# Cross-attention: V's parts in one stationary operand, four context products a step

## The chip, the cores and the metric

One core of a Trainium2 chip runs the whole kernel as one program. The time is the device time of one execution in microseconds (us), as the median of several. Of the engines, PE is TensorE (matrix products; PEld is its loading of the stationary operand), DVE is VectorE, ACT is ScalarE, POOL is GpSimd, and SP issues most of the DMAs.

## The reference

A decoder block on x of 32 sequences x 256 tokens x 256 columns: self-attention, cross-attention to a context of 120 tokens, and a mixture of 16 experts, each followed by a residual sum and a layer norm. The change touches cross-attention alone:

```
q = einsum('bsd,dhk->bshk', x, Wq);  k, v = the same of ctx with Wk, Wv      # 16 heads of 64
logits  = einsum('bthk,bfhk->bhft', k, q * 64**-0.5)
weights = softmax(logits, axis=-1)
ctx     = einsum('bhft,bthk->bfhk', weights, v)
out     = einsum('bfhk,hkd->bfd', ctx, Wo)
```

## The kernel before

Every fp32 product is computed from rounded parts. A value is split into a high part (its copy in the format that PE reads, made by ACT) and a low part (the value minus the high part, made by DVE), and `three` (L127 to L131) replaces one product by three: high by high, low by high and high by low. In the trace these are lines L129, L130 and L131.

**Stages.** Self-attention comes first, cross-attention second, the experts last. Cross-attention works in steps: a step g is one pair of heads of one sequence, so there are 8 steps (NP) a sequence and 256 in all. The step's work is software-pipelined over slots: in slot m each engine does, for several different steps, the part that is due there. The offsets are written out by hand (L872): queries and keys at m - 2 (QL), scores and exponentials at m - 4 (SL), reciprocal and normalisation at m - 5 (IL), transposes of the probabilities at m - 6 (TL), the context product at m - 8 (CL), the output product at m - 10 (OL). One slot a step, so the length of a slot is what 256 steps cost. The functions `tensor`, `scalar`, `vector`, `gpsimd` and `sync` inside `cross_attention` each hold a `slot(J, m)`: it issues that engine's instructions of slot m in this order, and an engine runs them in that order. A body has 32 slots (four sequences) and runs eight times. The first slots of the stage lie among the last ones of self-attention, and the last ones among the first work of the experts.

**What a slot holds beside the steps' own work.** Keys are computed for two sequences at once, so the key products (six), ACT's and DVE's two key passes each (on partitions 0 to 63 and 64 to 127) stand in eight slots of sixteen only. V is projected in slots 1 and 2 of each eight (six products of 512 columns each). The residual, the norm, the transposes of x and x2 and the gate have their places by m modulo 8, and each body has the choice of tokens (softmax over experts, four rounds of the eight largest).

**The context product before.** V lies in SBUF as `v_hi` and `v_lo` (L806), for each pair of heads 64 columns of head 0, 64 of zeros and 64 of head 1. A window of 128 columns holds head 0 and zeros, or zeros and head 1; with it as stationary operand and the transposed probabilities `pT_hi`, `pT_lo` (256 columns) as moving one, the two heads' three products each (six in all, L1079) add up in one region of the bank `CX`, `CX[:, 0:T]`, in which head 0 has partitions 0 to 63 and head 1 has 64 to 127. PE starts them when the low part of step g - 1 has been read from `CX` (`cxlo_done`, L1076). ACT copies `CX` to `c_hi` (L1180), DVE subtracts that from `CX` to make `c_lo` (L1286), both in slot g + 8, and PE's output product reads both in slot g + 10 (L1117).

**Order in a slot.** PE: V projection, scores, transposes of x, keys and queries, context product, transposes of the probabilities, x2 transposes, gate, output product. ACT: xT, `v_hi`, `q_hi`, `k_hi`, `c_hi`, `pT_hi`, x2T, gate, four exponentials with their sums (L1206). DVE: xT, `v_lo` (L1249), residual (L1256), maximum (`ca_shift`, L1262), reciprocal (`ca_inverse`, L1268), `q_lo` (L1275), `k_lo` (L1279), `c_lo`, `pT_lo` (L1291), x2, statistics, the choice of tokens. The bank of queries and keys is single: PE's next queries wait for `q_lo` and `k_lo` of the step before.

## Time and profile before

| | us |
|---|---|
| median of three runs | 3175.88 (3175.04 to 3178.29) |
| profiled execution: its span, first to last instruction | 3171.4 |
| PE busy | 3088.7 (97%) |
| DVE busy | 2256.1 (71%) |
| ACT busy | 2142.4 (68%) |
| POOL busy | 1581.9 (50%) |

The page gives the profiled execution by its span; what lies around the span isn't in it (the median of the runs is 4.5 us above it). Busy time is the union of an engine's instructions. On DVE and ACT an instruction's recorded time includes a tail in which the next one already runs, so what an instruction costs in a row of them is the distance from its start to the next one's start, which is shorter than its own time. On PE likewise: products overlap in the records, and the distance of their starts is their cost.

### The profile page before, as it was taken

How to read it: one execution, taken by the hardware profiler on the slowest of the kernel's cores; microseconds unless marked ns; L12 is line 12 of the kernel's file. 1: busy time of each engine (PE TensorE's matmuls, PEld its weight loads, DVE VectorE, ACT ScalarE, POOL GpSimd, SP SyncE). 2: the span in 40 equal slices, each digit the busy share in tenths (PEclk: the TensorE clock that was granted, in tenths of full speed). 3: DMA queues.
4: the chain of work that ended last, by engine and by line, in shares of the span. 5: the costliest groups of instructions: out<-in, count | busy, mean ns of one | idle time of the engine just before them, and what ended most of it. 6: DMA issues, size and time to landing. Idle time of an engine off the chain costs nothing. (4 is left out here: it accounts for less than half of the span.)

```text
span 3171.4 us, 78666 instructions
## 1 busy us (share of the span) xinstructions
PE 3088.7 (97%) x22624; PEld 2900.2 (91%) x22624; DVE 2256.1 (71%) x6566; ACT 2142.4 (68%) x6930; POOL 1581.9 (50%) x2904
## 2 busy tenths in 40 slices
PE   6999999999999998999999999999989999999998
PEld 5999999999999987999999999999868888889998
DVE  6777777777877877778877778787745455544665
ACT  6888888888887877787877877777734444442222
POOL 3666766766676765333333333333446666653000
PEclk8999999999999999999999999999989999999999
DMA  6444444444444440121111111111245444533333
GB/s 181 117 120 125 127 125 121 121 120 122 127 111 111 125 143 24 48 64 45 54 55 45 57 55 44 64 45 48 94 118 119 100 98 101 128 56 85 120 124 106
DMA packets 193684, 300.70 MB, mean 95 GB/s; under 512 B 33856, under 2 KB 134080, under 8 KB 192704
## 3 DMA queue, kind: packets, MB, share of 16 engines
q1 hardware_dynamic: 168768, 262.91, 27.8%
q0 software_dynamic: 24576, 33.57, 6.2%
q8 instruction: 176, 2.88, 0.4%
q14 instruction: 164, 1.34, 0.1%
HBM read 116.02 MB, written 67.11 MB: 58 GB/s over the span
## 5 line engine op out<-in xcount | busy, mean ns | idle before, releaser
L964 POOL TENSOR_SCALAR ca_prob<-ca_prob,ca_inverse 128x120 f32<-128x120 f32 x1024 | 354.6, 365 | 632.5 <-DVE ca_inverse L1268 630.5
L665 ACT ACTIVATE sa_prob<-sa_prob,sa_shift 128x128 f32<-128x128 f32 (+1 forms) x1024 | 453.6, 461 | 2.6 <-DVE sa_shift L718 2.6
L1206 ACT ACTIVATE ca_prob<-bank,ca_shift 128x120 f32<-128x120 f32 x1024 | 353.7, 366 | 6.0 <-DVE ca_shift L1262 3.5
L460 POOL TENSOR_SCALAR sa_prob<-sa_prob,sa_inverse 128x128 f32<-128x128 f32 x512 | 198.5, 388 | 234.5 <-DVE sa_inverse L726 220.4
L718 DVE CUSTOM_DVE_ANT_0 sa_prob<-bank,sa_mask 128x128 f32<-128x128 f32 (+1 forms) x1024 | 304.7, 352 | 6.9 <-PE bank L138 2.7
L136 PE MATMUL bank<-sa_ow,sa_y_hi 128*128 128x256 f32 x1024 | 279.6, 304 | 0.0
L136 PE MATMUL bank<-sa_kvT_a,sa_q 128*128 128x128 f32 (+1 forms) x1024 | 251.7, 281 | 17.7 <-DMA sa_q<-sa_q_tile 17.4
L138 PE MATMUL bank<-sa_kvT_b,sa_q 112*128 112x128 f32 (+1 forms) x1024 | 261.6, 281 | 0.0
L749 DVE TENSOR_TENSOR sa_pT_lo<-bank,sa_pT_hi 128x384 fp32r<-128x384 f32 x512 | 258.3, 544 | 1.8 <-ACT sa_pT_hi L650 1.8
L138 PE MATMUL bank<-sa_ow,sa_y_lo 112*128 112x256 f32 x1024 | 258.8, 283 | 0.0
L462 POOL TENSOR_SCALAR sa_prob<-sa_prob,sa_inverse 128x256 f32<-128x256 f32 x512 | 244.9, 478 | 0.0
L1824 ACT ACTIVATE ex_act_g<-bank 128x512 f32<-128x512 f32 x128 | 76.5, 598 | 239.5 <-PE bank L131 226.0
L1677 POOL DMA_INDIRECT mid_acc<-ex_out,ex_to_tokens x112 | 191.1, 1706 | 88.1 <-DVE ex_out L1939 56.3
L742 DVE TENSOR_TENSOR sa_y_lo<-bank,sa_y_hi 96x512 fp32r<-96x512 f32 x256 | 175.1, 684 | 71.8 <-ACT sa_y_hi L642 61.6
L650 ACT ACTIVATE sa_pT_hi<-bank 128x384 fp32r<-128x384 f32 x512 | 223.2, 494 | 3.1 <-PE bank L565 2.9
L642 ACT ACTIVATE sa_y_hi<-bank 128x512 fp32r<-128x512 f32 x256 | 153.0, 598 | 99.0 <-PE bank L131 99.0
L1206 ACT ACTIVATION_READ_ACCUMULATOR ca_prob<-bank,ca_shift 128x1 f32 x1024 | 219.4, 214 | 0.0
L136 PEld LDWEIGHTS bank<-sa_kvT_a,sa_q 128*128 128x128 f32 x1024 | 197.5, 193 | 19.1 <-issue 18.1
L565 PE MATMUL bank<-all_ident,sa_prob 128*128 128x128 f32 x1536 | 211.4, 274 | 3.0 <-POOL sa_prob L462 2.9
L1906 DVE TENSOR_TENSOR ex_hid<-ex_act_g,bank 128x512 f32<-128x512 f32 x128 | 87.8, 686 | 175.0 <-PE bank L131 165.3
L665 ACT ACTIVATION_READ_ACCUMULATOR sa_prob<-sa_prob,sa_shift 128x1 f32 x1024 | 210.7, 206 | 0.0
L731 DVE SCALAR_TENSOR_TENSOR sa_q_tile<-bank,sa_qbias,sa_q_tile 128x512 fp32r<-128x512 f32 x144 | 107.7, 748 | 142.4 <-ACT sa_q_tile L633 142.3
(259 smaller groups left out, 12014.1 us busy)
## 6 DMA issues: line engine op xcount, KB each, us to landing
sa_q<-sa_q_tile SPq DMA_DIRECT2D x128, 288.0 KB
sa_q<-sa_q_tile SPq DMA_DIRECT2D x160, 112.0 KB
mid_x2T<-ca_x2T SPq DMA_DIRECT2D x32, 512.0 KB, 3.0
ex_sx<-mid_x2T SPq DMA_DIRECT2D x32, 512.0 KB, 3.3
sa_q<-sa_q_tile SPq DMA_DIRECT2D x304, 32.0 KB, 3.0
sa_xT_raw<-in_xT SPq DMA_DIRECT2D x32, 256.0 KB, 2.8
sa_q<-sa_q_tile SPq DMA_DIRECT2D x32, 256.0 KB
sa_x_res<-in_x SPq DMA_DIRECT2D x32, 256.0 KB, 2.8
```

What stands on the lines that cost most here:

```text
L136: pe.matmul(out, stat_hi, mov_hi, start=start, stop=False, skip_group_check=True)
L138: return pe.matmul(out, stat_lo[rows], mov_lo[rows], start=False, stop=stop, skip_group_check=True)
L460: pool.tensor_scalar(prob[:, r, hh, 0:P], prob[:, r, hh, 0:P], inverse[:, r, 2 * hh:2 * hh + 1], 1.0, ALU.mult, ALU.mult)
L462: pool.tensor_scalar(prob[:, r, hh, P:3 * P], prob[:, r, hh, P:3 * P], inverse[:, r, 2 * hh + 1:2 * hh + 2], 1.0, ALU.mult, ALU.mult).then ...
L565: mm = pe.transpose(TR[hh][:, n * P:n * P + P], prob[:, r, hh, n * P:n * P + P], ident[:])
L650: act.activation(pT_hi[:, r, hh], TR[hh][:, 0:3 * P], ACT.Copy).then_inc(pThi_done, 1)
L665: act.activation(prob[:, r, hh, cols], prob[:, r, hh, cols], ACT.Exp, bias=shift[:, r, n:n + 1], scale=-1.0, accum_out=total[:, r, n:n + 1 ...
L718: dve.tensor_tensor_reduce(out=prob[:, r, hh, cols], in0=SC[hh][:, t * T:t * T + (t + 1) * P], in1=mask[:].rearrange("p a s -> p (a s)")[: ...
L749: dve.tensor_tensor(pT_lo[:, r, hh], TR[hh][:, 0:3 * P], f32(pT_hi[:, r, hh]), ALU.subtract).then_inc(pTlo_done, 1)
L964: ins = pool.tensor_scalar(prob[:, r, t, hh], prob[:, r, t, hh], inverse[:, r, n:n + 1], 1.0, ALU.mult, ALU.mult)
L1206: act.activation(prob[:, r, t, hh], SC[g % 2][:, n * S:n * S + S], ACT.Exp, bias=shift[:, r, n:n + 1], accum_out=total[:, r, n:n + 1]).the ...
L1677: pool.indirect_dma_start(d["acc"].rearrange("b t c -> (b t) c"), bass.IndirectOffsetOnAxis(ap=of[:, j:j + 1], axis=0), out[:, i, t], None ...
```

## The change

V's four parts of a pair of heads lie in one tensor `v`, side by side: high part of head 0, low of head 0, low of head 1, high of head 1, 64 columns each, without zeros. One stationary operand of 128 columns holds high and low part of one head; it is multiplied with `pT_hi` and with `pT_lo`. So there are two products a head, four a step. The two halves of the result lie on different partitions, head 0 in columns 0 to 255 of `CX` and head 1 in columns 256 to 511. ACT copies the whole of `CX` (512 columns) to a new tensor `cx`. DVE then makes two sums on 64 partitions each, of one half from `CX` and the other half from `cx`, into a new tensor `c`. At the head of the next slot ACT rounds `c` to `c_hi` and DVE subtracts, `c_lo = c - c_hi`, now with both inputs in SBUF. PE's next context product waits for the sums (`csum_done`), its output product for `c_lo` (`chalf_lo`). ACT makes `v`'s high parts in one pass of 512 columns and DVE its low parts in one, where there were two of 256 columns. GpSimd no longer writes the zeros of V.

```diff
@@ -56,6 +56,7 @@
 MASKED = -3e38
 SELF_SCALE = float(C // H) ** -0.5
 CROSS_SCALE = float(DH) ** -0.5
+PAST_LOW = 576
 
 
 Later = namedtuple("Later", "own base")
@@ -803,7 +804,10 @@
     xT_hi, xT_lo = al.split("xT", [P, 2, KC, T])
     q_hi, q_lo = al.split("q", [P, RING, T])
 
-    v_hi, v_lo = al.split("v", [S, 2, NP, 3 * DH])
+    al.sb("v_before", [P, PAST_LOW])
+    cx = al.sb("cx", [P, 2, 2 * T])
+    al.sb("v_between", [P, 4 * T - PAST_LOW])
+    v = al.sb("v", [S, 2, NP, 4, DH], F32R)
     k_hi, k_lo = al.split("k", [P, 2, NP, 2 * S])
     prob = al.sb("prob", [P, RING, TT, 2, S])
     shift = al.sb("shift", [P, RING, TT * 2])
@@ -829,6 +833,7 @@
     var_eps, rstd = al.sb("var_eps", [P, TT]), al.sb("rstd", [P, TT])
 ...
+    c = al.sb("c", [P, 2, T])
 
     XT, M, QK, SC, TR, CX, O = *bank[0:3], bank[3:5], *bank[5:8]
 
@@ -858,7 +863,8 @@
     s_mm, max_done, exp_done = al.sem("s_mm"), al.sem("max_done"), al.sem("exp_done")
     inv_done, p_done = al.sem("inv_done"), al.sem("p_done")
     p_tr, pThi_done, pTlo_done = al.sem("p_tr"), al.sem("pThi_done"), al.sem("pTlo_done")
-    cx_mm, cxhi_done, cxlo_done = al.sem("cx_mm"), al.sem("cxhi_done"), al.sem("cxlo_done")
+    cx_mm, cxcopy_done, csum_done = al.sem("cx_mm"), al.sem("cxcopy_done"), al.sem("csum_done")
+    chalf_hi, chalf_lo = al.sem("chalf_hi"), al.sem("chalf_lo")
 ...
@@ -936,12 +942,11 @@
             pool.wait_ge(cross.o_mm, B * NP)
             pool.wait_ge(cross.w_lo, KC * (len(CROSS) - 1))
             pool.memset(half[:], -0.5).then_inc(const, 1)
-            zeros = [k_hi[0:DH, :, :, S:2 * S], k_lo[0:DH, :, :, S:2 * S], k_hi[DH:P, :, :, 0:S], k_lo[DH:P, :, :, 0:S],
-                     v_hi[:, :, :, DH:2 * DH], v_lo[:, :, :, DH:2 * DH]]
+            zeros = [k_hi[0:DH, :, :, S:2 * S], k_lo[0:DH, :, :, S:2 * S], k_hi[DH:P, :, :, 0:S], k_lo[DH:P, :, :, 0:S]]
             for n, t in enumerate(zeros):
                 pool.wait_ge(const, n + 1)
                 pool.memset(f32(t), 0.0).then_inc(const, 1)
-            pool.wait_ge(const, 7)
+            pool.wait_ge(const, 5)
 ...
@@ -987,7 +992,7 @@
 
     def tensor(pe):
 
-        first_use = {1: (cross.w_lo, KC), QL: (cross.w_lo, KC * (len(CROSS) - 1)), SL: (const, 5), QL + 1: (cross.o_read, B), CL: (const, 7),
+        first_use = {1: (cross.w_lo, KC), QL: (cross.w_lo, KC * (len(CROSS) - 1)), SL: (const, 5), QL + 1: (cross.o_read, B),
                      OL: (cross.w_lo, KC * (len(CROSS) - 1) + 1), GATE: (gate_done, 1)}
 
         def slot(J, m):
@@ -1073,11 +1078,12 @@
                 if p == 0:
                     need(pe, vlo_done, upto_seq(J, g // NP, 2))
                 need(pe, pTlo_done, upto(J, g))
-                need(pe, cxlo_done, upto(J, g - 1))
+                need(pe, csum_done, upto(J, g - 1, 2))
                 for hh in range(2):
-                    win = slice(hh * DH, hh * DH + 2 * DH)
-                    mm = three(pe, CX[:, 0:T], v_hi[:, b, p, win], v_lo[:, b, p, win], pT_hi[:, r, hh], pT_lo[:, r, hh],
-                               hh == 0, hh == 1)
+                    both = v[:, b, p, 2 * hh:2 * hh + 2].rearrange("s a k -> s (a k)")
+                    out = CX[:, hh * T:(hh + 1) * T]
+                    pe.matmul(out, both, pT_hi[:, r, hh], start=True, stop=False, skip_group_check=True)
+                    mm = pe.matmul(out, both, pT_lo[:, r, hh], start=False, stop=True, skip_group_check=True)
                 mm.then_inc(cx_mm, 1)
             g = m - TL
             if step_exists(J, g):
@@ -1114,7 +1120,7 @@
             g = m - OL
             if step_exists(J, g):
                 r, p = g % RING, g % NP
-                need(pe, cxlo_done, upto(J, g))
+                need(pe, chalf_lo, upto(J, g))
                 if p == 0:
                     need(pe, o_read, upto_seq(J, g // NP - 1))
                 for t in range(TT):
@@ -1128,6 +1134,11 @@
 
     def scalar(act):
         def slot(J, m):
+            g = m - CL - 1
+            if step_exists(J, g):
+                need(act, csum_done, upto(J, g, 2))
+                need(act, o_mm, upto(J, g - RING))
+                act.activation(c_hi[:, g % RING], c[:, g % 2], ACT.Copy).then_inc(chalf_hi, 1)
             if m % (2 * NP) == 0 and seq_exists(J, m // NP):
                 pr = m // (2 * NP)
                 need(act, c_in, upto_pair(J, pr, 32))
@@ -1154,10 +1165,8 @@
                 need(act, v_mm, upto_seq(J, b, 2, n - 1))
                 if n == 0:
                     need(act, cx_mm, upto(J, (b - 1) * NP - 1))
-                for hh in range(2):
-                    ins = act.activation(v_hi[:, b % 2, n * NP // 2:(n + 1) * NP // 2, hh * 2 * DH:hh * 2 * DH + DH],
-                                         v_bank(J, b, n)[0:S, :].rearrange("s (p h k) -> s p h k", h=2, k=DH)[:, :, hh], ACT.Copy)
-                ins.then_inc(vhi_done, 1)
+                act.activation(v[:, b % 2, n * NP // 2:(n + 1) * NP // 2, 0:4:3],
+                               v_bank(J, b, n)[0:S, :].rearrange("s (p h k) -> s p h k", h=2, k=DH), ACT.Copy).then_inc(vhi_done, 1)
             g = m - QL
             if step_exists(J, g):
                 r, b, p = g % RING, (g // NP) % 2, g % NP
@@ -1174,10 +1183,9 @@
                     ins.then_inc(khi_done, 1)
             g = m - CL
             if step_exists(J, g):
-                r = g % RING
                 need(act, cx_mm, upto(J, g))
-                need(act, o_mm, upto(J, g - RING))
-                act.activation(c_hi[:, r], CX[:, 0:T], ACT.Copy).then_inc(cxhi_done, 1)
+                need(act, csum_done, upto(J, g - 2, 2))
+                act.activation(cx[:, g % 2], CX[:], ACT.Copy).then_inc(cxcopy_done, 1)
             g = m - TL
             if step_exists(J, g):
                 r = g % RING
@@ -1226,6 +1234,10 @@
 
     def vector(dve):
         def slot(J, m):
+            g = m - CL - 1
+            if step_exists(J, g):
+                need(dve, chalf_hi, upto(J, g))
+                dve.tensor_tensor(c_lo[:, g % RING], c[:, g % 2], f32(c_hi[:, g % RING]), ALU.subtract).then_inc(chalf_lo, 1)
             if m % (2 * NP) == 0 and seq_exists(J, m // NP):
                 need(dve, chi_done, upto_pair(J, m // (2 * NP)))
                 dve.tensor_tensor(cT_lo[:], cT_raw[:], f32(cT_hi[:]), ALU.subtract).then_inc(clo_done, 1)
@@ -1244,11 +1256,9 @@
                 if isinstance(J, int) and J == 0 and m == 1:
                     dve.wait_ge(cross.o_mm, B * NP)
                 need(dve, vhi_done, upto_seq(J, b, 2, n - 1))
-                for hh in range(2):
-                    at = (slice(None), b % 2, slice(n * NP // 2, (n + 1) * NP // 2), slice(hh * 2 * DH, hh * 2 * DH + DH))
-                    ins = dve.tensor_tensor(v_lo[at], v_bank(J, b, n)[0:S, :].rearrange("s (p h k) -> s p h k", h=2, k=DH)[:, :, hh],
-                                            f32(v_hi[at]), ALU.subtract)
-                ins.then_inc(vlo_done, 1)
+                of = v[:, b % 2, n * NP // 2:(n + 1) * NP // 2]
+                dve.tensor_tensor(of[:, :, 1:3], v_bank(J, b, n)[0:S, :].rearrange("s (p h k) -> s p h k", h=2, k=DH),
+                                  f32(of[:, :, 0:4:3]), ALU.subtract).then_inc(vlo_done, 1)
             if m % NP == NORM % NP and seq_exists(J, (m - NORM) // NP):
                 b = (m - NORM) // NP
                 need(dve, o_mm, upto(J, (b + 1) * NP - 1))
@@ -1281,9 +1291,12 @@
                     ins.then_inc(klo_done, 1)
             g = m - CL
             if step_exists(J, g):
-                r = g % RING
-                need(dve, cxhi_done, upto(J, g))
-                dve.tensor_tensor(c_lo[:, r], CX[:, 0:T], f32(c_hi[:, r]), ALU.subtract).then_inc(cxlo_done, 1)
+                need(dve, cxcopy_done, upto(J, g))
+                need(dve, chalf_lo, upto(J, g - 2))
+                for hh in range(2):
+                    own, other = slice(hh * DH, (hh + 1) * DH), slice((1 - hh) * DH, (2 - hh) * DH)
+                    dve.tensor_tensor(c[own, g % 2], CX[other, hh * T:(hh + 1) * T], cx[own, g % 2, hh * T:(hh + 1) * T],
+                                      ALU.add).then_inc(csum_done, 1)
             g = m - TL
             if step_exists(J, g):
                 r = g % RING
```

## Rows read from the trace of the kernel before

**Rows 1.** The page: busy time of the engines; the granted clock in 40 slices.

```profile
PE 3088.7 (97%) x22624; PEld 2900.2 (91%) x22624; DVE 2256.1 (71%) x6566; ACT 2142.4 (68%) x6930; POOL 1581.9 (50%) x2904
...
PEclk8999999999999999999999999999989999999999
```

**Rows 2.** Windows of the stage (stretch, length, busy of engines, clock, DMA share, GB/s).

```profile
1350.00:2154.00 804.00, 798.91 (x6574) 776.35 (x6573) 639.59 (x1715) 638.83 (x2483) 281.49 (x790) 1.00 0.16 52
1240.00:2290.00 1050.00, 1042.53 (x8576) 1012.63 (x8574) 833.13 (x2213) 836.14 (x3243) 377.62 (x1046) 1.00 0.17 55
```

**Rows 3.** Waits, 1350 to 2154 us (who waited for whom: total, times, longest).

```profile
ACT ca_q_hi L1166 <- PE bank L131: 115.3, 136, 1.4
DVE ca_q_lo L1275 <- ACT ca_k_hi L1172: 69.2, 78, 1.7
DVE ca_v_lo L1249 <- ACT ca_v_hi L1158: 41.8, 42, 1.5
...
PE bank L129 <- ACT ca_prob L1206: 5.1, 5, 1.3
```

**Rows 4.** Groups of DVE and ACT, 1350 to 2154 us (count, busy, mean ns, idle before).

```profile
L1286 DVE TENSOR_TENSOR ca_c_lo<-bank,ca_c_hi 128x256 fp32r<-128x256 f32 x192 | 80.8, 421 | 11.8 <-ACT ca_c_hi L1180 7.3
...
L1180 ACT ACTIVATE ca_c_hi<-bank 128x256 fp32r<-128x256 f32 x191 | 73.3, 384 | 30.9 <-PE bank L131 28.4
```

**Rows 5.** Timeline of PE (start, us): first of six context products, then transposes.

```profile
1629.63 0.29 PE L129 MATMUL bank<-ca_pT_hi,ca_v_hi 120*128 120x256 f32 x1
...
1630.34 0.60 PE L1089 MATMUL bank<-all_ident,ca_prob 128*120 128x128 f32 x4
```

**Rows 6.** Timeline of DVE in a slot with keys.

```profile
1617.81 0.42 DVE L1275 TENSOR_TENSOR ca_q_lo<-bank,ca_q_hi 128x256 fp32r<-128x256 f32 x1 [0.44 <-ACT ca_k_hi L1172]
1618.15 0.81 DVE L1279 TENSOR_TENSOR ca_k_lo<-bank,ca_k_hi 64x240 fp32r<-64x240 f32 x2
1618.99 0.42 DVE L1286 TENSOR_TENSOR ca_c_lo<-bank,ca_c_hi 128x256 fp32r<-128x256 f32 x1
1619.34 0.68 DVE L1291 TENSOR_TENSOR ca_pT_lo<-bank,ca_pT_hi 120x512 fp32r<-120x512 f32 x1
1619.93 0.68 DVE L1314 TENSOR_TENSOR ca_x2T<-bank,ca_x2T 128x512 fp32r<-128x512 f32 x1
```

**Rows 7.** Timeline of DVE: V's two low parts; the chosen tokens' columns, by partitions.

```profile
1607.45 0.76 DVE L1249 TENSOR_TENSOR ca_v_lo<-bank,ca_v_hi 120x256 fp32r<-120x256 f32 x2 [1.48 <-ACT ca_v_hi L1158]
1608.12 0.68 DVE L1256 TENSOR_TENSOR ca_res<-bank,ca_x_res 128x512 f32<-128x512 f32 x1
...
1661.89 0.18 DVE L1370 COPY all_weight_of<-bank 32x16 f32 x1
1661.98 0.23 DVE L1372 TENSOR_SCALAR all_token_of<-bank,ca_first_token 32x16 f32 x1
1662.22 0.18 DVE L1370 COPY all_weight_of<-bank 32x16 f32 x1
```

**Rows 8.** Timeline of ACT: from the context's copy to the exponentials' end.

```profile
1630.87 0.39 ACT L1180 ACTIVATE ca_c_hi<-bank 128x256 fp32r<-128x256 f32 x1
1631.15 0.59 ACT L1186 ACTIVATE ca_pT_hi<-bank 120x512 fp32r<-120x512 f32 x1
1631.63 0.36 ACT L1206 ACTIVATE ca_prob<-bank,ca_shift 128x120 f32<-128x120 f32 x1
...
1632.97 0.63 ACT L1143 ACTIVATE ca_xT_hi<-bank 128x512 fp32r<-128x512 f32 x1
```

**Rows 9.** Timeline of DVE in a slot without keys.

```profile
1655.35 0.42 DVE L1286 TENSOR_TENSOR ca_c_lo<-bank,ca_c_hi 128x256 fp32r<-128x256 f32 x1 [0.27 <-ACT ca_c_hi L1180]
...
1657.63 0.66 DVE L1262 TENSOR_REDUCE ca_shift<-bank 128x4 f32<-128x480 f32 x1 [0.94 <-PE bank L131]
```

**Rows 10.** Windows at the end of self-attention, in which the clock fell.

```profile
1162.00:1165.50 3.50, 0.85 (x5) 0.41 (x4) 1.77 (x11) 0.96 (x6) 3.19 (x8) 1.00 0.89 264
1165.50:1172.30 6.80, 5.70 (x25) 5.61 (x26) 1.96 (x6) 3.33 (x11) 1.25 (x3) 0.50 1.03 399
```

## The prediction, made before the changed kernel was timed

> **What bounds the kernel now.** I read the busy line and the clock first: PE is busy 97% of the span, at full clock but for a few slices [rows 1]. The change lies in one stage, so I then cut out that stage. From 1240 to 2290 us PE is busy 1042.5 of 1050 us at a clock of 1.00 [rows 2], and the longest sum of PE's own waits is 5.1 us in 804 [rows 3]. PE sets the pace. But the other two aren't far: in 804 us that hold 192 steps [rows 2, 4], a step takes 4.19 us, of which PE is busy 4.16, DVE 3.33 and ACT 3.33. So DVE and ACT have 0.86 us of room a step each, and this is the number that decides. The waits say what kind of idle time that room is: DVE waits 69 us for `k_hi` and 42 us for `v_hi`, and ACT waits 115 us for the query products [rows 3]. That is waiting for input from PE, in the slots in which PE has extra products. It isn't room that DVE can use whenever it likes.
>
> **PE: two products of six go.** The six start at 1629.63 and the transposes behind them at 1630.34: 0.71 us, 0.118 each [rows 5]. The four that stay have the same shape (120 rows of 128, 256 columns moving), so a step loses 0.24 us and PE needs 4.19 - 0.24 = 3.95. If nothing else moved, 256 steps would give 61 us.
>
> **DVE: one pass becomes three.**
> - The old `c_lo` goes, 1618.99 to 1619.34, 0.35 us [rows 6].
> - The new `c_lo` is as wide but reads two SBUF tensors. Its price in SBUF isn't in these rows; passes from the bank of the same width cost 0.34 and 0.35 [rows 6]. I take the same, between 0.30 and 0.42 (its whole recorded time, nothing overlapped). So the two cancel.
> - Two sums of 64 partitions by 256 columns come. The nearest row is the pair of `k_lo`, also 64 partitions each, also first 0 to 63 and then 64 to 127: from 1618.15 to the next start at 1618.99, 0.84 us for 2 x 240 columns [rows 6]. Two passes on 120 partitions that don't change partitions take less, 0.67 for 2 x 256 (`v_lo`, 1607.45 to 1608.12) [rows 7]. So the price of such a pair hangs not on the elements but on the step from one set of partitions to another. The small writes of the chosen tokens say the same: on one set of 32 partitions the next instruction starts 0.09 us behind, and where the set changes 0.24 us behind, when the one before has ended [rows 7]. The sums change partitions twice in a slot, like `k_lo`, so I take 0.84 plus 16 columns each at (0.68 - 0.42)/256, about 1 ns a column: 0.87 us. Bounds: 0.67 (as `v_lo`) and 0.95 (each its full time and a little more, since input and output of one instruction start at different partitions, which no row shows).
> - V's low parts in one pass of 512 columns cost as `pT_lo`, 0.59 [rows 6], for 0.67 [rows 7]: 0.08 less, twice in eight steps, 0.02 a step.
>
> Sum: 3.33 - 0.35 + 0.35 + 0.87 - 0.02 = 4.18 us of busy DVE a step, and 3.98 to 4.33 between the bounds. In steps without keys the same change of partitions newly falls behind `q_lo`. The Trainium skill ("VectorE: DVE Perf Modes", "Two Vector instructions with no wait between them") says that a Vector instruction starts only when all earlier ones have finished if its output, or its first input from SBUF or PSUM, starts in another group of 32 partitions than the last one did. The pairs in [rows 7] agree (0.09 and 0.24). It speaks against this change: it makes all passes around the sums dear, and by it `q_lo` too would be held in half of the steps, 0.08 more there, so that the sum would be 4.22 instead of 4.18.
>
> **ACT.** The copy grows from 256 to 512 columns: from 0.28 (1630.87 to 1631.15) to 0.48 (as `pT_hi`, 1631.15 to 1631.63) [rows 8]. The rounding of `c` is a pass more, 0.28. V's high parts in one pass save 0.02. Sum: 3.33 + 0.20 + 0.28 - 0.02 = 3.79; bounds 3.70 to 3.90 (recorded times instead of distances). ACT stays below PE's 3.95.
>
> **GpSimd** writes no zeros for V, once, before the first context product. Nobody is late for it: cost nothing on either side. SBUF and DMAs keep their order; SP's queue isn't touched.
>
> **The sum.** PE 3.95, DVE 4.18, ACT 3.79, against a step of 4.19. PE's saving is real and DVE takes its place as the bound, at a work that is nearly the length of the old step. A busy DVE isn't a DVE without idle time, and here is where I choose. Recorded tails make the 4.18 a little too large (ahead of each idle gap stands the tail of the last pass, 0.07 us for `c_lo`, 0.42 recorded against 0.35 to the next start [rows 6]; with one such gap a step, 4.11 is the hard floor, and I take 4.15). Against this stands idle time that can't be filled. In slots with the V projection PE has six products of 512 columns more, and DVE waits for `v_hi`, up to 1.5 us, 1.0 us in the mean of 42 waits [rows 3]. DVE can come late from the slot before and so use part of that: how late is set by the single banks. PE's next queries need `k_lo` at once, its next context product needs the sums, its next transposes need `pT_lo`; I take half a microsecond in slots without keys (there DVE waits 0.94 us before the maximum today [rows 9], less the longer copy) and a quarter or less in those with. So of the 1.0 us about half stays idle, in a quarter of the slots: 0.12 a step. The long slots of DVE (statistics, and the choice of tokens, of which the columns alone take four times the 0.33 us from 1661.89 to 1662.22 [rows 7]) exceed PE's and delay PE directly. The work's 4.15 plus 0.12 gives 4.27 a step.
>
> What is queued behind the new waits: at the head of a slot DVE now waits for ACT's `c_hi`, which ACT issues only behind its four exponentials (1.34 us, 1631.63 to 1632.97 [rows 8]) and only when DVE's sums are done. Behind that wait on DVE stand `v_lo`, the residual and the maximum, and the next exponentials wait for the maximum. The loop is `c_hi` 0.39, `c_lo` 0.42, maximum 0.66, exponentials 1.34: 2.8 us with the recorded times [rows 4, 6, 8, 9], shorter than any step, so it costs nothing in plain slots.
>
> 4.27 - 4.19 = 0.08 us a step. Of 256 steps I count 250 (the first and last ones lie among other work). 0.08 x 250 = 20 us. The profiled execution's span of 3171.4 would become 3191; the median of the runs is 4.5 above that span: 3195 to 3196, I say 3195.
>
> **The rivals.**
> - PE stays the bound. If the sums cost 0.67 or less and overlap as `v_lo`, DVE needs 3.98, beside PE's 3.95; with the V slots' idle time filled this is a step of 4.05 to 4.13: 15 to 35 us faster, 3141 to 3161. For it: PE has all its work ready, and 0.24 us is 6% of a step. Against it: `k_lo`. Chance 0.22, with all cases down to 3170.
> - It evens out. DVE at 4.18 to 4.20 with next to no idle time: 3170 to 3182. Chance 0.18. That is also what would be seen if the two products were saved and all of it lost to a full DVE.
> - My forecast, DVE is the bound with some idle time: 4.22 to 4.40 a step, 3182 to 3228, likeliest 3195. Chance 0.48.
> - The wait at the head of the slot makes ACT and DVE take turns. It decides once ACT's exponentials end later than DVE's `pT_lo` and extras: in slots with a fifth ACT pass (x2T, gate, xT) and keys. Each such slot then loses up to `c_hi`'s 0.39; in half of the slots that is 0.2 a step on top of my 4.27: 3195 + 50 = 3245. Chance 0.08.
> - The clock. It fell to 0.50 after 3.5 us in which PE was busy for 0.85 us, and stayed there for 6.8 us, with 5.7 busy [rows 10]. In the stage PE has no such gap today. The choice of tokens adds 1.3 us or more to DVE (four times 0.33 [rows 7]) in a slot in which PE could be short of work. One fall a body, 3.4 us at half speed, is 14 to 27 us more: 3209 to 3222. Chance 0.04.
>
> The Trainium skill ("SBUF — State Buffer", "SBUF: two separate sides") has another rule against the change: a VectorE instruction with two SBUF inputs and a GpSimd one that reads SBUF exclude each other. The new `c_lo` is of that kind. In numbers of this case: POOL is busy 281.5 of 804 us in 790 instructions [rows 2], 35% of the time and 0.36 us each. If they met by chance, 0.35 x 0.36/2 = 0.06 us a step, 16 us more, or some 3211, within the forecast's range; but `c_lo` comes after `pT_lo`, when the multiplies behind the reciprocal should be over. No row of the stage shows it; I give it 0.03 as the case by itself that moves the time up, out of the forecast's share.
>
> **How the numbers follow.** Chances: faster by over 0.2% (6.4 us, about what can be told from no change here) 0.22; within it 0.18; slower 0.48 + 0.08 + 0.04 = 0.60. The range leaves out about 0.1 on each side: from 3150 (a step of 4.09, just under DVE's floor) to 3236 (a step of 4.43, the upper bound of DVE's work and 0.1 of idle time). The likeliest case's own range is 3182 to 3228.
>
> **What would show it.** In the profile after, in the same stage: PE busy no longer 99% but 92 to 96%, with waits for the sums, `k_lo` or `pT_lo`; DVE busy 96% or more of the step and 4.1 to 4.2 us of it; ACT 3.8 us. The pair of sums, with the next start behind it, 0.84 to 0.90 us. PE's four products 0.47. DVE waits at `c_lo` for ACT's `c_hi` would be the turn-taking rival. I am wrong on the side of faster if the sums overlap (0.67) or DVE can run later behind PE than half a microsecond, and the step is then nearer to PE's 3.95.

## The result, and the profile after

The changed kernel takes 3211.85 us in the median (3210.27 to 3213.2), the kernel before 3176.52 beside it: a ratio of 1.0111 (95% interval 1.0097 to 1.0126), 35.3 us slower. The forecast was slower, 3195, so the sign and the range hold and the size is about half of what came. A second comparison on another chip gave 1.0123 (1.0107 to 1.014), 38.6 us; the experiments below are set against that one.

The page after, with the two lines that answer to [rows 1]:

```profile
span 3208.9 us, 78973 instructions
...
PE 3079.1 (96%) x22112; PEld 2854.2 (89%) x22112; DVE 2453.9 (76%) x7014; ACT 2256.4 (70%) x7122; POOL 1585.8 (49%) x2902
...
DVE  6787777777787778999999999999955555554565
...
PEclk8999999999999999999999999999989999999999
```

PE has 512 products fewer and only 9.6 us less busy time; DVE has 198 us more and now shows 9 tenths through nearly the whole stage, as PE did before. The stage's windows and groups, as in [rows 2, 4]:

```profile
1240.00:2330.00 1090.00, 1033.20 (x8082) 966.46 (x8082) 1030.00 (x2658) 951.68 (x3439) 381.81 (x1046) 1.00 0.17 54
1350.00:2154.00 804.00, 764.50 (x6000) 715.20 (x6000) 761.17 (x1978) 701.72 (x2548) 274.70 (x764) 1.00 0.16 51
...
L1298 DVE TENSOR_TENSOR ca_c<-bank,ca_cx 64x256 f32<-64x256 f32 x372 | 157.1, 422 | 11.8
L1304 DVE TENSOR_TENSOR ca_pT_lo<-bank,ca_pT_hi 120x512 fp32r<-120x512 f32 x186 | 128.7, 692 | 5.7
L1240 DVE TENSOR_TENSOR ca_c_lo<-ca_c,ca_c_hi 128x256 fp32r<-128x256 f32 x185 | 77.2, 417 | 3.6 <-ACT ca_c_hi L1141 3.2
```

The 372 sums are 186 steps, against 192 in the same 804 us before: a step takes 804/186 = 4.32 us, not 4.19. DVE is busy 761.17/186 = 4.09 of it, ACT 3.77, PE 4.11. PE's 4.11 isn't its work: 764.50 us for 6000 products are 0.127 us each, against 0.122 before (798.91 for 6574). I take the difference for pauses too short to show as idle time, since a product ahead of a pause is recorded to its end. Read the waits beside [rows 3]: DVE has all but stopped waiting for ACT (the 69 us for `k_hi` and the 42 for `v_hi` are 8.7 and nothing), and ACT's longest wait and PE's are now for DVE.

```profile
ACT ca_prob L1214 <- DVE ca_shift L1272: 38.3, 56, 1.4
ACT ca_q_hi L1175 <- PE bank L132: 31.5, 64, 1.2
...
PE bank L130 <- DVE ca_k_lo L1289: 12.9, 18, 1.0
...
PE bank L130 <- DVE ca_q_lo L1285: 9.1, 22, 0.6
...
DVE ca_q_lo L1285 <- ACT ca_k_hi L1181: 8.7, 35, 0.4
```

DVE's timeline in a slot without keys (start, us), to be set against [rows 6, 9]:

```profile
1653.23 0.39 DVE L1285 TENSOR_TENSOR ca_q_lo<-bank,ca_q_hi 128x256 fp32r<-128x256 f32 x1
1653.65 0.87 DVE L1298 TENSOR_TENSOR ca_c<-bank,ca_cx 64x256 f32<-64x256 f32 x2
1654.56 0.69 DVE L1304 TENSOR_TENSOR ca_pT_lo<-bank,ca_pT_hi 120x512 fp32r<-120x512 f32 x1
```

The pair of sums takes 0.91 us to the next start, and `q_lo` ahead of it 0.42, where it takes 0.31 in such slots of the kernel before (mean of 54): nothing overlaps on either side of a change of partitions.

The clearest picture is one that I worked out from the traces: the distance of each `q_lo`'s start on DVE from the one before it, averaged over the six bodies of steps 32 to 223. The first eight columns lead to steps with keys, the next eight to steps without (the second half of the 32 slots is much the same, but for the choice of tokens that is in it). The third line is DVE's idle time in the same stretches of the kernel before:

```
            with keys                                   without keys                             mean of 32
before      5.62 4.03 3.94 4.36 4.37 4.39 4.31 5.28     4.79 3.14 2.71 3.50 4.04 4.62 4.09 3.47     4.20
after       4.54 4.94 4.30 4.25 3.94 4.10 4.51 4.69     5.11 4.20 3.57 3.52 3.03 5.05 4.92 3.60     4.36
idle before 2.14 0.22 0.51 0.95 1.56 1.44 0.80 1.71     0.70 0.18 0.00 0.66 1.76 0.67 0.21 0.82     0.86
```

Over all 32, steps with keys went from 4.56 to 4.48 and steps without from 3.85 to 4.24. Look at the third line: the four stretches in which DVE had 0.22 us or less of idle time grew by 0.83 to 1.06 us, about the full price of the sums, and those in which it had 0.95 to 2.14 us got shorter. Two pairs of neighbouring stretches of the kernel before show it in its own records, the first of the tenth and eleventh columns, the second of the fifth and sixth (length, then busy time of PE, PEld, DVE, ACT and POOL):

```profile
1645.30:1651.15 5.85, 5.85 (x53) 5.85 (x52) 5.67 (x19) 5.01 (x21) 3.47 (x9) 1.00 0.16 45
1622.19:1630.88 8.69, 8.69 (x76) 8.45 (x75) 5.76 (x16) 6.70 (x28) 3.18 (x10) 1.00 0.33 95
```

DVE is busy 5.67 us of 5.85 in one and 5.76 of 8.69 in the other. Between the stage's first and last `q_lo` the changed kernel takes 36.4 us more, of the 37.5 by which the two profiled spans differ; other stages play next to no part.

### The profile page after: what moved, and what is told of

The parts are those of the page before. It is cut to its first block and busy times, and to the rows that moved or that the text cites. A ratio compares the mean times of both kernels' runs of the same rounds, so it can differ in the third digit from the quotient of the medians.

```text
span 3208.9 us, 78973 instructions
## 1 busy us (share of the span) xinstructions
PE 3079.1 (96%) x22112; PEld 2854.2 (89%) x22112; DVE 2453.9 (76%) x7014; ACT 2256.4 (70%) x7122; POOL 1585.8 (49%) x2902
## 5 line engine op out<-in xcount | busy, mean ns | idle before, releaser
L1298 DVE TENSOR_TENSOR ca_c<-bank,ca_cx 64x256 f32<-64x256 f32 x512 | 216.2, 422 | 16.5 <-ACT ca_cx L1188 0.4
```

Source lines behind the costliest of these rows:

```text
L1298: dve.tensor_tensor(c[own, g % 2], CX[other, hh * T:(hh + 1) * T], cx[own, g % 2, hh * T:(hh + 1) * T], ALU.add).then_inc(csum_done, 1)
```

## The experiments

All times are medians, and each difference is against the kernel before on the same chip (3172.95, 3173.69 and 3173.79 us for the three groups of runs). Two theories stood against each other. A: DVE is full, its amount of work sets the step. B: the rounding a slot later makes ACT and DVE take turns at the head of the slot.

**The sums alone, in the kernel before.**

```diff
@@ kernel before, vector, g = m - CL
                 need(dve, cxhi_done, upto(J, g))
+                for hh in range(2):
+                    own, other = slice(hh * DH, (hh + 1) * DH), slice((1 - hh) * DH, (2 - hh) * DH)
+                    dve.tensor_tensor(c[own, g % 2], CX[other, 0:T], f32(c_hi[own, r]), ALU.add)
                 dve.tensor_tensor(c_lo[:, r], CX[:, 0:T], f32(c_hi[:, r]), ALU.subtract).then_inc(cxlo_done, 1)
```

> The kernel before, with its six products, plus two sums on 64 partitions and 256 columns each on DVE ahead of each c_lo (their result isn't used). PE and ACT do exactly the work of before. If DVE's amount of work alone makes the loss, DVE goes from 3.33 to 4.2 us a step here too, in a kernel in which PE needs 4.16: the step becomes 4.4 to 4.6, 3230 to 3280, the changed kernel's loss plus a good part of what the four products gave it. If the loss comes from the new order and the new waits (rounding a slot later), the added sums fit into DVE's idle 0.86 us: 3176 to 3190.

3239.63, ratio 1.0204 (1.0187 to 1.0221), 65.9 us slower. PE and ACT do what they did before, no wait is added, and the step is 4.47. A part of it is the clock of TensorE. Once in five of the eight bodies, in the slots with the choice of tokens, PE stands still for 2.4 to 2.8 us, and soon after the granted clock is at 0.50 for 3.4 us. In the changed kernel PE's longest pauses there are 1.1 to 1.4 us, and the clock doesn't fall. One such place (order as above):

```profile
1614.30:1616.90 2.60, 0.00 (x1) 0.00 (x0) 2.54 (x8) 1.92 (x9) 1.38 (x4) 1.00 0.01 3
1618.20:1621.60 3.40, 3.40 (x18) 3.40 (x18) 2.66 (x8) 1.36 (x3) 0.43 (x2) 0.50 0.01 2
```

The bodies with a fall take 143.5 us in the mean and the first full one, without, 141.1; in the changed kernel, which has no fall in any of them, the same bodies differ by 0.6. My estimate from these numbers is 1.8 us a fall, 9 us of the 65.9. The other 57 are the main finding: some 0.9 us of DVE work a step (the pair takes 0.86 to the next start, `q_lo` ahead of it 0.42 and not 0.31), offered to an engine with 0.86 us of idle time a step, costs 0.22 us a step. The idle time took in only three quarters of it.

**Six products again, in the changed kernel.**

```diff
                     pe.matmul(out, both, pT_hi[:, r, hh], start=True, stop=False, skip_group_check=True)
+                    pe.matmul(out, both, pT_lo[:, r, hh], start=False, stop=False, skip_group_check=True)
                     mm = pe.matmul(out, both, pT_lo[:, r, hh], start=False, stop=True, skip_group_check=True)
```

> The changed kernel with a third product for each head again (a repeated low one, six a step; the output is slightly off the reference's for it). PE does 0.24 us more a step, DVE and ACT the same. If DVE sets the pace everywhere, it costs little: below 3225. If PE sets it in part of the slots (those with V's projection and those with keys), the 60 us come back in that part: 3235 to 3255. If PE sets it everywhere: 3270.

3237.53, ratio 1.0198 (1.0181 to 1.0215), 63.8 us slower than before and so 25 us slower than the changed kernel (38.6). The two products that the change saves are thus worth 25 of the 61 us that they take on PE, and that includes the clock, which fell in five bodies of this run too; at 1.8 us a fall, again as an estimate, some 9 us of the 25 are that, and 16 are left. Put beside the run above it also gives the rest of the change: the whole change except the saved products costs 63.8, the sums alone cost 65.9. Beside the sums, the copy of 512 columns, ACT's extra pass and the later rounding together cost nothing that can be told.

```profile
1350.00:2154.00 804.00, 776.06 (x6210) 743.28 (x6209) 742.95 (x1975) 604.32 (x2340) 265.26 (x743) 0.99 0.16 50
```

```profile
1350.00:2154.00 804.00, 777.93 (x6194) 742.35 (x6195) 742.96 (x1922) 679.88 (x2469) 266.77 (x743) 0.99 0.16 50
```

The same window of the two runs: first the kernel before with the sums, then the changed one with six products. PE is busy alike within 2 us and DVE to the hundredth of one, and ACT has 75 us more in the second without any effect.

**ACT's rounding left out.**

```diff
@@ scalar
-                act.activation(c_hi[:, g % RING], c[:, g % 2], ACT.Copy).then_inc(chalf_hi, 1)
@@ vector, head of the slot
-                need(dve, chalf_hi, upto(J, g))
-                dve.tensor_tensor(c_lo[:, g % RING], c[:, g % 2], f32(c_hi[:, g % RING]), ALU.subtract).then_inc(chalf_lo, 1)
+                need(dve, csum_done, upto(J, g, 2))
+                dve.tensor_tensor(c_lo[:, g % RING], cx[:, g % 2, 0:T], f32(c_hi[:, g % RING]), ALU.subtract).then_inc(chalf_lo, 1)
@@ vector, g = m - CL: the sums write c_hi[own, g % RING], and wait for the output product of step g - RING
```

> ACT's rounding of c is left out: DVE's two sums write c_hi themselves, and the low part is taken from cx, a pass of the same shape with two SBUF inputs, without waiting for ACT (the output isn't the reference's). DVE's work is unchanged, ACT does 0.31 us less a step and the wait at the head is gone. A: the step stays at 4.2 to 4.33: 3190 to 3212. B: the turns end, PE or DVE with little idle time sets the pace: 3150 to 3180.

3215.19, ratio 1.0136 (1.0119 to 1.0153), 42.2 us slower than before, 3.6 more than the changed kernel and just above what A gave. ACT's busy time in the window falls from 701.7 to 650.8 us and the time doesn't follow. Theory B falls for the changed kernel: with DVE full, neither ACT's work nor the wait at the head of the slot sets the pace.

**The low part behind the maximum.**

```diff
@@ vector: the block "g = m - CL - 1" with c_lo moves from the head of the slot
                 dve.reciprocal(inverse[:, r], total[:, r]).then_inc(inv_done, 1)
+            g = m - CL - 1
+            if step_exists(J, g):
+                need(dve, chalf_hi, upto(J, g))
+                dve.tensor_tensor(c_lo[:, g % RING], c[:, g % 2], f32(c_hi[:, g % RING]), ALU.subtract).then_inc(chalf_lo, 1)
```

> The changed kernel with DVE's low part of the context moved from the head of the slot to behind the maximum and the reciprocal; all is computed and no engine's work changes. If what is left of idle time on DVE (0.2 us a step) is its wait for ACT's c_hi with the maximum queued behind it, this gives it back: 3175 to 3195. If DVE's work sets the pace, the order matters little: 3203 to 3215.

3224.25, ratio 1.0162 (1.0145 to 1.0179): 12 us slower than the changed kernel, a miss of both guesses. The order costs something, but in the other direction than B says. I didn't follow up why; among the distances that grew are the last ones of the eights without keys, which hold V's first half (3.86 and 3.94 us for 3.60).

**One pass in place of the two sums.**

```diff
-                for hh in range(2):
-                    own, other = slice(hh * DH, (hh + 1) * DH), slice((1 - hh) * DH, (2 - hh) * DH)
-                    dve.tensor_tensor(c[own, g % 2], CX[other, hh * T:(hh + 1) * T], cx[own, g % 2, hh * T:(hh + 1) * T],
-                                      ALU.add).then_inc(csum_done, 1)
+                dve.tensor_tensor(c[:, g % 2], CX[:, 0:T], cx[:, g % 2, T:2 * T], ALU.add).then_inc(csum_done, 2)
```

> Theory A (VectorE is full: its passes, the two sums on 64 partitions above all, set the step of 4.33 us) against theory B (the wait at the head of the slot for ACT's c_hi makes ACT and DVE take turns, and DVE's amount of work doesn't matter). Here the two sums on 64 partitions are replaced by one pass on 128 partitions and 256 columns, which adds the wrong halves: the output isn't the reference's. A: the pair's 0.90 us becomes 0.34, DVE falls to 3.6 us a step, and PE sets the pace with its 3.95 to 4.05: 3110 to 3140. B: the loop of c_hi, c_lo, maximum and exponentials is untouched: 3195 to 3212.

3151.98, ratio 0.9934 (0.9917 to 0.995), 21 us faster than before and 60 faster than the changed kernel. The direction is A's, the size isn't: PE was to set a pace of 3.95 to 4.05, and the step is 4.10. One wait has grown from the 3.2 us that it has in the changed kernel:

```profile
DVE ca_c_lo L1240 <- ACT ca_c_hi L1141: 57.1, 106, 1.0
```

Where DVE isn't full, it does wait for ACT at the head of the slot, in about half of the steps and 0.29 us a step in the mean. That is the wait of theory B. No run has one sum and leaves this wait out, so what it costs isn't shown.

**Two passes that don't change partitions.**

```diff
-                (the two sums, as above)
+                dve.tensor_tensor(cx[:, g % 2, 0:T], CX[:, T:2 * T], cx[:, g % 2, 0:T], ALU.add).then_inc(csum_done, 1)
+                dve.tensor_tensor(c[:, g % 2], CX[:, 0:T], cx[:, g % 2, T:2 * T], ALU.add).then_inc(csum_done, 1)
```

> Two passes again, each of 256 columns from bank and SBUF, but both on all 128 partitions, so that no start partition changes (the first writes its sum back into cx, the second adds the wrong halves: the output isn't the reference's). This tells the number of passes from the change of partitions. If the change of partitions is what makes the pair dear, the pair takes 0.66 to 0.70 us and the pass before it 0.34 in place of 0.42, DVE falls to 3.85 to 3.9 a step: 3130 to 3160, faster than the kernel before. If only the passes count, the pair stays at 0.85 to 0.90: 3205 to 3212. Theory B: 3195 to 3212.

3171.57, ratio 0.9994 (0.9985 to 1.0004), equal to before and 40 us faster than the changed kernel, though not the 3130 to 3160 that I expected. As many passes, twice as many partitions, the same columns; only the start partitions stay. DVE's timeline (start, us):

```profile
1652.38 0.39 DVE L1285 TENSOR_TENSOR ca_q_lo<-bank,ca_q_hi 128x256 fp32r<-128x256 f32 x1
1652.69 0.41 DVE L1296 TENSOR_TENSOR ca_cx<-bank,ca_cx 128x256 f32<-128x256 f32 x1
1653.02 0.41 DVE L1297 TENSOR_TENSOR ca_c<-bank,ca_cx 128x256 f32<-128x256 f32 x1
1653.35 0.67 DVE L1302 TENSOR_TENSOR ca_pT_lo<-bank,ca_pT_hi 120x512 fp32r<-120x512 f32 x1
```

The pair takes 0.66 us here and 0.91 in the changed kernel, and `q_lo` 0.31 against 0.42: the steps from one set of partitions to another cost 0.36 us in such a slot (0.25 in one with keys, where the pass ahead was held before), and 40 us in the whole. That is more than the change lost.

**Four products, then two.** To see what held the step at 4.10 in the run with one sum, I took another two products from it.

```diff
@@ as in the run with one sum, and
-                    pe.matmul(out, both, pT_hi[:, r, hh], start=True, stop=False, skip_group_check=True)
-                    mm = pe.matmul(out, both, pT_lo[:, r, hh], start=False, stop=True, skip_group_check=True)
+                    mm = pe.matmul(out, both, pT_hi[:, r, hh], start=True, stop=True, skip_group_check=True)
```

> As e1_one_sum (one pass in place of the two sums), and also only two context products a step, that by pT_lo left out (the output isn't the reference's): PE does 0.24 us less a step than in e1. In e1 the shortest slots with keys took 3.94 us, the same as before, though PE had 0.24 us less to do. If these slots are held by the loop through the single bank of queries and keys (products, ACT's passes, DVE's passes, next products), they stay at 3.9 here too, and the whole gains only in slots without keys and with the V projection: 3125 to 3145. If PE's work is what holds them, they go to 3.7 and the whole to 3090 to 3105.

3129.78, ratio 0.9858 (0.9842 to 0.9875), 43.9 us faster than before and 22.9 faster than with four products, of 61 that PE saved. The distances, worked out as above:

```
            with keys                                   without keys                             mean of 32
one sum     4.55 4.42 3.94 4.26 4.02 4.10 4.52 4.69     5.12 3.47 3.06 3.21 3.24 4.59 4.22 3.60     4.11
+ two prod. 4.30 4.42 3.94 4.25 3.93 3.96 4.52 4.26     5.11 3.48 3.05 3.21 3.04 4.39 4.22 3.60     4.04
```

The shortest distance with keys stays at 3.93 to 3.94 with six products (before), four and two. The timeline of the last run shows the loop that holds them (all engines; start, us):

```profile
1611.90 0.34 PE L130 MATMUL bank<-ca_cT_hi,cross_wk_hi 128*128 128x240 f32 x1
...
1613.22 0.28 PE L132 MATMUL bank<-ca_xT_hi,cross_wq_lo 128*128 128x256 f32 x1
...
1613.54 0.38 ACT L1174 ACTIVATE ca_q_hi<-bank 128x256 fp32r<-128x256 f32 x1
...
1613.82 0.73 ACT L1180 ACTIVATE ca_k_hi<-bank 64x240 fp32r<-64x240 f32 x2
...
1614.58 0.42 DVE L1284 TENSOR_TENSOR ca_q_lo<-bank,ca_q_hi 128x256 fp32r<-128x256 f32 x1
...
1614.92 0.81 DVE L1288 TENSOR_TENSOR ca_k_lo<-bank,ca_k_hi 64x240 fp32r<-64x240 f32 x2
...
1615.79 0.38 PE L130 MATMUL bank<-ca_cT_hi,cross_wk_hi 128*128 128x240 f32 x1
```

Each line starts within 0.06 us of the end of the one that it needs: twelve products, three ACT passes, three DVE passes, and then the single bank of queries and keys is free for the next step, 3.89 us later. The same hand-over, from `k_lo`'s end to the next key product, takes 0.08 us in the mean in the slot of 3.94 us of the kernel before. So the loop was closed there already, although PE's records fill the time and show no wait, and PE's saving had nothing to shorten.

The loop isn't all. With two products it is closed in nearly every slot with keys; with four only in the second and third of each eight, and in the others 0.24 to 0.54 us pass between `k_lo` and the next key product. And stretches without keys stay as long too (3.21 and 3.60 us in both rows), as does the 4.52 with keys. In these ACT has next to no idle time left, here in the run with two products (ACT is the fourth busy time):

```profile
1614.58:1619.11 4.53, 4.53 (x40) 4.42 (x39) 3.85 (x10) 4.49 (x16) 1.38 (x4) 1.00 0.00 0
1634.99:1638.19 3.20, 3.20 (x30) 3.17 (x29) 2.90 (x8) 3.20 (x14) 1.39 (x4) 1.00 0.57 193
```

So ACT's wider copy and its extra pass, which cost nothing beside a full DVE, seem to be part of what holds the step once DVE has room. That is read from busy times; I made no run with one sum and less work for ACT.

**The low part on GpSimd.** The aim here was a kernel that computes everything and beats both.

```diff
@@ vector, head of the slot: the block with c_lo is removed
@@ gpsimd, behind the normalisation of the probabilities
+            g = m - CL - 1
+            if step_exists(J, g):
+                need(pool, chalf_hi, upto(J, g))
+                pool.tensor_tensor(c_lo[:, g % RING], c[:, g % 2], f32(c_hi[:, g % RING]), ALU.subtract).then_inc(chalf_lo, 1)
```

> The low part of the context is taken by GpSimd and not by DVE, at the end of its slot, everything else as in the changed kernel; all is computed. GpSimd has 2.8 us of room a step and a pass of 128 x 256 with two SBUF inputs takes it 0.73 us. A: DVE loses 0.34 us a step and falls to 3.8, ACT stays at 3.8, PE's 3.95 sets the pace again: 3120 to 3155, faster than both kernels. B would give much the same, since DVE's wait at the head goes too. If GpSimd's later low part delays PE's output product, or its passes and DVE's block each other, 3170 or more.

3193.58, ratio 1.0066 (1.005 to 1.0083): 18 us faster than the changed kernel, still 20.6 slower than before, and a miss of my 3120 to 3155. Part of it was the end of the stage, where GpSimd's queue holds the first gathers. With DVE taking those last nine:

```diff
@@ gpsimd
-            if step_exists(J, g):
+            if step_exists(J, g) and not (isinstance(J, int) and J == BODIES):
@@ vector, head of the slot
+            if step_exists(J, g) and isinstance(J, int) and J == BODIES:
+                need(dve, chalf_hi, upto(J, g))
+                need(dve, chalf_lo, upto(J, g - 1))
+                dve.tensor_tensor(c_lo[:, g % RING], c[:, g % 2], f32(c_hi[:, g % RING]), ALU.subtract).then_inc(chalf_lo, 1)
```

> As e3_pool_low, but in the last nine slots of the stage, in which GpSimd waits for and issues the experts' first gathers, DVE takes the low part as in the changed kernel; all is computed. In e3 the stage's steps were 4.23 us, which by themselves should have given 3180, and the time from the last query split to the experts' first product of gates was 8 to 12 us longer than in the other runs. If GpSimd's queue in the tail is what ate it: 3172 to 3183. If not, as e3: 3190 to 3195.

3184.89, ratio 1.0035 (1.0021 to 1.005), 2 us above what I expected: the queue in the tail was worth 9 us. The best complete version of the new form is 27 us faster than the changed kernel and 11 slower than the kernel before. Moving x2's scaling to GpSimd as well was meant to shorten a long slot of DVE:

```diff
@@ gpsimd, ahead of the low part; removed from vector but for the last slots
+                need_alone(pool, rstd_done, upto_seq(J, b), spare_pool)
+                need_alone(pool, x2_out[b % 2], upto_pair(J, b // 2 - 1, 32), spare_pool)
+                for t in range(TT):
+                    ins = pool.tensor_scalar(x2[:, b % 2, t], res[:, t], meanvar[:, t, 0:1], rstd[:, t:t + 1],
+                                            ALU.subtract, ALU.mult)
+                ins.then_inc(x2_done, 1)
```

> As e9_pool_low_tail, and GpSimd also takes x2, the last scaling of the norm (two passes a sequence, which take DVE 0.64 us in one slot of eight), except in the last slots; all is computed. DVE's slot after the statistics gets shorter by 0.64, in the mean 0.08 us a step. If DVE's long slots still set the pace: 3165 to 3180. If GpSimd's two passes of 0.7 us delay its normalisation of the probabilities, for which PE's transposes wait: 3185 to 3200.

3233.13, ratio 1.0187 (1.017 to 1.0204), 59.3 us slower than before and a miss of both guesses. I had priced the two passes at 0.7 us each, from other GpSimd passes of that size. The group, and who waits for it:

```profile
L977 POOL TENSOR_SCALAR ca_x<-ca_res,ca_meanvar,ca_rstd 128x256 f32<-128x256 f32 x46 | 56.0, 1224 | 0.0
...
PEld bank L1115 <- POOL ca_x L977: 25.2, 23, 1.6
...
DVE ca_c L1312 <- POOL ca_c_lo L983: 21.1, 11, 1.9
```

They take 1.22 us each with two values by partition, and PE's transposes of x2 and DVE's next sums stand behind them. The granted clock also fell to 0.50 ten times within the stage, for 3.4 us each.

**The changed kernel again**, so that the last group has it on the same chip:

> The changed kernel itself once more, on the same chip as the other two, so that they are compared with it there: 3205 to 3215.

3212.38, as told above.

## Why the prediction was right, and where it was short

- **PE, 3.95 us of work.** The two products are gone at the price read (the four that stay take 0.46 us, 1651.27 to 1651.73), but the step that would have followed from them alone isn't there to be had. The run with one sum has PE's 3.95 and a DVE with room, and takes 4.10. I took "the sum of PE's work" as the floor of a step. The loop through the single bank holds some slots with keys at 3.94, ACT is full in others, and DVE waits for `c_hi`; I had read PE's 99% busy as work without a pause, which those records can't show.
- **The sums, 0.87 us, from the pair of `k_lo`.** They take 0.91 (1653.65 to 1654.56), 0.04 more. Going by the nearest row of the same kind and not by the number of elements was the step that decided the sign: at `v_lo`'s price I would have forecast no change or faster. The run with two wide passes shows this price itself: 0.66 for the pair, and 3171.57. What the Trainium skill says ("VectorE: DVE Perf Modes", "Two Vector instructions with no wait between them") held also where I left it out of the sum: `q_lo` ahead of a sum takes 0.42, for 0.31 before and in the run with wide passes, which is 0.11 where I had 0.08.
- **DVE, 4.18 us a step; ACT, 3.79.** Measured 4.09 and 3.77 by busy time. But the 0.87 us for the sums was a distance of starts and held the gaps of 0.03 us at each change of partitions, and these are idle time in the page: 11.8 us ahead of the sums and 5.7 ahead of `pT_lo` in the stage's groups above, 0.09 us a step. With them DVE's work is the 4.18 of the sum. The 0.03 that I took off for recorded tails was too much.
- **The idle time, 0.12 us a step: the right size by luck.** A step is 4.32 us with 4.09 busy, so 0.23 stay idle, and without the gaps 0.14. The prediction put its 0.12 wholly into the slots with V's products, as half of DVE's wait for `v_hi`. That wait is gone altogether: 42 us before, 0.4 us of idle time ahead of `v`'s low part after. What stands in its place is 8.7 us for `k_hi`, 3.2 for `c_hi`, and 10 us in which DVE waits for its own results, in the statistics and in the choice of tokens. So this mechanism was wrong and its number close.
- **What 3195 lacks of 3211.85.** In this window 4.32 for 4.27, 0.03 of work and 0.02 of idle time. In the mean of whole bodies it is 4.36, with 4.12 busy and 0.24 idle, against 4.20 before: 0.15 us more a step and not 0.08. What I left out is how unevenly DVE's idle time lies. I compared means, and DVE had next to none in the stretches where PE's work was short; there the sums cost their full price, and PE's saving in the others doesn't make that good. The sums put into the kernel before show this without the rest of the change: about 0.22 us a step, clock taken out by estimate, where the means (4.2 of work for DVE, a step of 4.19) would have let them cost almost nothing.
- **The rivals.** "PE stays the bound" and "it evens out" fell with the sums' price. "Take turns" fell by the run without rounding, for this kernel; with one sum its wait is there. The clock stayed at 1.00 from 1240 us to the stage's end, with one fall of 6.8 us at 1231 us; but the rival as it was put, one fall a body of 3.4 us, came in the runs with the sums alone and with six products, where PE's pauses were longer. For the shared access to SBUF the stage gives a small sign and its end a larger one, below; neither is in the sum.
- **What would show it.** PE busy 95% (92 to 96 was said), though with short pauses in it. PE's waits are for `k_lo`, as said, and for `q_lo`, hardly for the sums or `pT_lo`. The pair takes 0.91, just above the 0.84 to 0.90 said. DVE 94.7%, where 96 or more was said.

What stays open: why the low part behind the maximum costs 12 us, how the 4.10 of the run with one sum divides between the loop, ACT's work and the wait for `c_hi`, and how much of the run with GpSimd's low part (4.23 us a step, with DVE at 725.67 of 804 us busy) is DVE's uneven slots and how much the longer way of `c_lo` through another engine.

## What to carry to other kernels

An idle share read as a mean is no room: compare the engines stretch by stretch. Here stretches in which DVE had 0.22 us or less of idle time took the full 0.9 us of new work as time, whatever it had elsewhere; engines that hand single buffers to each other averaged little of a short slot against a long one. Before a saving on the bound engine is credited in full, look for what would hold the slot at the same length: here the loop of products, ACT, DVE and back through one bank in 3.89 us of 3.94, and an ACT with next to no idle time. Read the clock in each experiment too, before its time is put down to the edit. And a trade of PE columns for VectorE passes must be priced by rows of the same partition pattern: two passes on 64 partitions each cost 0.91 us, two on all 128 with twice the elements 0.66.

## What the runs showed of the hardware

I hadn't expected to see VectorE held up beside GpSimd, but at the end of the stage it was, once, in the changed kernel:

```profile
2329.68 1.29 POOL L986 TENSOR_TENSOR next_w_lo<-next_w_raw,next_w_hi 128x512 fp32r<-128x512 f32 x1 [3.42 <-ACT next_w_hi L1231]
...
2330.03 1.21 DVE L1240 TENSOR_TENSOR ca_c_lo<-ca_c,ca_c_hi 128x256 fp32r<-128x256 f32 x1 [0.48 <-ACT ca_c_hi L1141]
```

`c_lo`, with both inputs in SBUF, took 1.21 us where its mean is 0.417; GpSimd's pass, also on SBUF, ended at 2330.97, and `c_lo` 0.27 us later. In the stage itself `c_lo` meets GpSimd's power of the variance: that took 797 to 819 ns in the 31 cases in which a `c_lo` ran beside it and 714 in the one without, and 701 in the mean before; `c_lo` itself kept its 0.42 us there. The Trainium skill ("SBUF — State Buffer", "SBUF: two separate sides") has this rule, that such instructions exclude each other. The first number agrees with it, as seen once; the second is a delay of 0.1 us and less than a whole `c_lo`, so it agrees in direction alone. GpSimd's scaling with two values by partition took 1.22 us for 128 x 256, against 0.74 for its `c_lo` of the same size.
